# A grouped 3x3 convolution behind three attention blocks: its input strips made by a tripled 1x1 convolution in place of shifted copies

## The reference, cut to what matters

```python
h = lax.conv_general_dilated(x, w1, (1, 1), 'SAME', ...) + b1          # 1x1, 64 -> 128 channels
h = jax.nn.relu(_bn(h, g1, be1, m1, v1))
h = lax.conv_general_dilated(h, w2, (1, 1), 'SAME', ...,
                             feature_group_count=32) + b2              # 3x3, 32 groups of 4 channels
h = jax.nn.relu(_bn(h, g2, be2, m2, v2))
out = lax.conv_general_dilated(h, w3, (1, 1), 'SAME', ...) + b3        # 1x1, 128 -> 64
return jax.nn.relu(out + x)
```

## Time and profile before

| | |
|---|---|
| median of three executions | 128.46 us |
| span of the profiled execution | 125.2 us |
| TensorE, matmul | 105.7 us busy, 84% |
| VectorE | 93.7 us, 75% |
| ScalarE | 68.5 us, 55% |
| GpSimd | 42.7 us, 34% |

### The profile page before, as it was taken

One profiled execution on the slowest core, in us unless ns is written; L12 is line 12 of the kernel. 1 busy time (PEld: TensorE's weight loads), 2 busy tenths in 40 slices (PEclk: granted clock), 3 DMA queues, 4 the chain that ended last, 5 costly groups with the idle time before them and its releaser, 6 DMA issues.

```text
span 125.2 us, 1845 instructions
## 1 busy us (share of the span) xinstructions
PE 105.7 (84%) x600; PEld 64.4 (51%) x600; DVE 93.7 (75%) x246; ACT 68.5 (55%) x164; POOL 42.7 (34%) x43
## 2 busy tenths in 40 slices
PE   4988999899999988599399957998697992998990
PEld 1475957577777775365035634985353530221350
DVE  1078999878888669737979989793878739998733
ACT  3137985687979775637503310025534579986530
POOL 8996004351608217095500079991000000000000
PEclk9999999999999999999999999999999999999999
DMA  3960000000000000000000000000000000000022
GB/s 105 309 280 0 0 0 0 5 5 0 0 0 0 0 5 0 0 0 0 5 0 0 0 3 0 0 0 0 0 0 0 0 5 3 0 0 0 5 84 84
DMA packets 1593, 2.81 MB, mean 22 GB/s; under 512 B 176, under 2 KB 1200, under 8 KB 1584
## 3 DMA queue, kind: packets, MB, share of 16 engines
q1 hardware_dynamic: 1152, 2.02, 4.5%
q10 hardware_dynamic: 432, 0.67, 1.6%
HBM read 2.17 MB, written 0.52 MB: 22 GB/s over the span
## 4 chain that ended last, share of the span: by engine, by line
PE 42%; DVE 29%; ACT 15%; issue 8%; DMA 2%; POOL 1%; ACTq 0%; DVEq 0%
PE bank L913 5%; DVE strips L307 5%; PE bank L883 4%; DVE probn L604 4%; ACT prob L411 4%; PE bank L1074 3%; PE bank L1104 3%; DVE ffh L253 3%; PE bank L1116 3%; PE bank L1052 3%; ACT strips L529 3%; DVE nmax L595 3%; DMA p<-in_p 2%; PE duo L1140 2%; DVE qkprod L738 2%
## 5 line engine op out<-in xcount | busy, mean ns | idle before, releaser
L411 ACT ACTIVATE prob<-bank,nmax 128x256 f32<-128x256 f32 x32 | 14.8, 469 | 8.2 <-DVE nmax L595 7.8
L883 PE MATMUL bank<-kz,q 128*128 128x256 f32 x64 | 16.4, 383 | 0.3 <-ACT kz L400 0.3
L595 DVE TENSOR_REDUCE nmax<-bank 128x2 f32<-128x512 f32 x16 | 11.0, 689 | 5.7 <-PE bank L883 5.7
L307 DVE COPY strips<-strips 32x480 f32<-32x480 f32 x32 | 12.8, 400 | 3.0 <-ACT strips L529 2.4
L883 PEld LDWEIGHTS bank<-kz,q 128*128 128x128 f32 x64 | 11.5, 190 | 2.1 <-issue 0.5
L604 DVE TENSOR_SCALAR probn<-prob,rrec 128x256 f32<-128x256 f32 x32 | 12.1, 421 | 0.6
L529 ACT ACTIVATE strips<-bank,bnsh 32x512 f32<-32x512 f32 x16 | 10.9, 680 | 2.1 <-PE duo L1140 1.1
L893 PE MATMUL bank<-pv,probn 128*128 128x128 f32 x64 | 10.0, 278 | 2.1 <-DVE probn L604 2.1
L501 ACT ACTIVATE sq<-bank,cb 128x512 f32<-128x512 f32 x4 | 2.7, 687 | 15.3 <-PE bank L1074 11.0
L1140 PE MATMUL duo<-strips,ctaps 128*32 128x512 f32 x72 | 8.3, 596 | 3.2 <-DVE strips L307 3.2
L893 PEld LDWEIGHTS bank<-pv,probn 128*128 128x128 f32 x64 | 7.4, 142 | 4.6 <-DVE probn L604 4.2
(11 more groups left out here) (148 smaller groups left out, 229.3 us busy)
## 6 DMA issues: line engine op xcount, KB each, us to landing
p<-in_p SPq DMA_DIRECT2D x1, 952.0 KB, 7.1
xT<-in_xT SPq DMA_DIRECT2D x4, 128.0 KB, 4.0
p<-in_p ACTq DMA_DIRECT2D x1, 448.0 KB, 5.7
out_dram<-xT SPq DMA_DIRECT2D x1, 256.0 KB, 2.0
out_dram<-xT SPq DMA_DIRECT2D x2, 128.0 KB, 1.7
pv<-in_pv ACTq DMA_DIRECT2D x1, 128.0 KB, 3.2
p<-in_p ACTq DMA_DIRECT2D x1, 79.5 KB, 3.0
```

What stands on the lines that cost most here:

```text
L307: return engine.tensor_copy(strips[32 * s:32 * s + 32, c % 2, r, :, 1:1 + SIDE, d], strips[32:64, c % 2, r, :, 1:1 + SIDE, f])
L411: s.activation(prob[:, n % 3, b, :], S_BANK[n % 3][:, b * TOK:(b + 1) * TOK], ACT.Exp, bias=nmax[:, n, b:b + 1], accum_out=rsum[:, n, b:b ...
L595: v.tensor_reduce(nmax[:, n, :], S_BANK[n % 3].rearrange("p (b m) -> p b m", b=BLK), AX.X, ALU.max, negate=True).then_inc(max_ready, 1)
L883: ins = mm(S_BANK[n % 3][:, b * TOK:(b + 1) * TOK], q[:, b * 128:b * 128 + 128], k, start=True, stop=True)
```

## The change

`conv1` now runs in 8 units (group `gr`, block `r`), each of six matmuls: for each `ty` of 0, 1, 2 and each image half `i`, 64 rows of input, 32 output columns (block `r`'s channels) into partitions `32 * ty` of the bank of half `i`. For `ty` 0 and 2 the input is shifted by one image row (16 positions), so 240 of each image's 256 positions are computed. The three partition groups of a bank hold the same channels seen from three rows. The 16 positions per image that no input reaches are filled once with -3e38 by two VectorE memsets in PSUM (`edges`), which the ReLU turns into zero. The strip is then written in one instruction of 96 partitions x 512: half 0 by ScalarE, half 1 by VectorE. `conv2` reads 96 partitions and goes over `tx`, the column, with rows of 16 floats in a pitch of 18. There are four strip buffers now, two of them in tiles of earlier stages. The orders of TensorE, ScalarE and VectorE change as shown.

```diff
-            g.memset(strips[:, :, :, :, :, :].rearrange("p a b c d e -> p (a b c d e)"), 0.0)\
+            g.memset(strips[:, :, :, :, :, 0:PAD:PAD - 1].rearrange("p a b c d e -> p (a b c d) e"), 0.0)\
                 .then_inc(zeroed, 1)
...
+            pool.wait_ge(avsum_sb, len(UNITS))
+            pool.wait_ge(pv_ps, NATT // 2)
+            for c in (2, 3):
+                g.memset(strip_of_chunk[c][:, :, :, :, 0:PAD:PAD - 1].rearrange("p r j a e -> p (r j a) e"), 0.0)\
+                    .then_inc(zeroed, 1)
...
+            def conv1_out(u):                                                  # ScalarE
+                act.wait_ge(c1_ps, u + 1)
+                if u % CONV_BLOCKS == 0:
+                    act.wait_ge(taps_ready, 1)
+                    act.wait_ge(zeroed, 3 if u == 0 else 5)
+                r = u % CONV_BLOCKS
+                s.activation(strip_of(u, 0), image_rows(conv1_bank(u, 0)[0:96, :]), ACT.Relu,
+                             bias=shift3[:, r:r + 1]).then_inc(c1_act, 1)
...
             conv1_out(0)
+            conv1_out(1)
             inverse_std(3)
-            conv1_out(1)
-            conv2_out(0)
             conv1_out(2)
             conv1_out(3)
+            conv2_out(0)
+            conv1_out(4)
+            conv1_out(5)
+            conv1_out(6)
             conv2_out(1)
+            conv1_out(7)
             conv2_out(2)
             conv2_out_last()
...
+            for r in range(CONV_BLOCKS):                                       # VectorE, after c1s
+                for ty in range(3):
+                    v.tensor_copy(shift3[32 * ty:32 * ty + 32, r:r + 1], bnsh[32 * r:32 * r + 32, 0:1])
...
+            def edges():
+                dve.wait_ge(ff_act, 2 * FH)
+                dve.wait_ge(ff_dve, 2 * FH)
+                rows = quad.rearrange("p (b a n) -> p b a n", b=4, a=2)
+                v.memset(rows[0:32, :, :, 0:SIDE], NOTHING)
+                v.memset(rows[64:96, :, :, TOK - SIDE:TOK], NOTHING).then_inc(edge_ps, 1)
+
+            def conv1_out(u):                                                  # VectorE
+                dve.wait_ge(c1_ps, u + 1)
+                if u % CONV_BLOCKS == 0:
+                    dve.wait_ge(zeroed, 3 if u == 0 else 5)
+                r = u % CONV_BLOCKS
+                v.tensor_scalar(strip_of(u, 1), image_rows(conv1_bank(u, 1)[0:96, :]), shift3[:, r:r + 1], 0.0,
+                                ALU.add, ALU.max).then_inc(c1_dve, 1)
...
             relu_ff(1)
+            edges()
             layer_norm(2)
-            shifts(0)
+            for u in range(CONV_BLOCKS):
+                conv1_out(u)
             layer_norm(3)
-            shifts(1)
-            shifts(2)
-            shifts(3)
+            for u in range(CONV_BLOCKS, 2 * CONV_BLOCKS):
+                conv1_out(u)
...
-            def conv1(c):
-                gr, i = c // 2, c % 2
+            def conv1(u):
+
+                gr, r = u // CONV_BLOCKS, u % CONV_BLOCKS
                 pe.wait_ge(ln_out, 3 + gr)
-                if c == 0:
+                if u == 0:
                     pe.wait_ge(taps_ready, 1)
-                    pe.wait_ge(ff_act, 4)
-                    pe.wait_ge(ff_dve, 4)
-                mm(bank[c], c1s[:, i, :], x2[:, gr, :], start=True, stop=True).then_inc(c1_ps, 1)
+                    pe.wait_ge(edge_ps, 1)
+                if u >= 2:
+                    pe.wait_ge(c1_act, u - 1)
+                    pe.wait_ge(c1_dve, u - 1)
+                for ty in range(3):
+                    to = slice(SIDE, TOK) if ty == 0 else slice(0, TOK - SIDE) if ty == 2 else slice(0, TOK)
+                    of = slice(0, TOK - SIDE) if ty == 0 else slice(SIDE, TOK) if ty == 2 else slice(0, TOK)
+                    for i in range(2):
+                        own = slice(64 * i, 64 * i + 64)
+                        o = conv1_bank(u, i)[32 * ty:32 * ty + 32, :].rearrange("p (j n) -> p j n", j=2)
+                        x = x2[own, gr, :].rearrange("p (j n) -> p j n", j=2)
+                        ins = mm(o[:, :, to], c1s[own, i, 32 * r:32 * r + 32], x[:, :, of],
+                                 start=True, stop=True)
+                ins.then_inc(c1_ps, 1)
...
-                pe.wait_ge(shifted, CONV_BLOCKS * (c + 1))
+                pe.wait_ge((c1_act, c1_dve)[c % 2], CONV_BLOCKS * (c // 2 + 1))
...
-                        ins = mm(bank[7 - c % 2][32 * r:32 * r + 32, :], ctaps[:, r, ty, :],
-                                 strips[:, c % 2, r, :, ty:ty + SIDE, :], start=ty == 0, stop=ty == 2)
+                        ins = mm(bank[7 - c % 2][32 * r:32 * r + 32, :], ctaps[0:96, r, tx, :],
+                                 strip_of_chunk[c][:, r, :, :, tx:tx + SIDE], start=tx == 0, stop=tx == 2)
...
             conv1(0)
+            conv1(1)
             variance(3)
-            conv1(1)
-            conv2(0)
             conv1(2)
             conv1(3)
+            conv2(0)
+            conv1(4)
+            conv1(5)
             conv2(1)
-            conv2(2)
+            conv1(6)
+            conv1(7)
             conv3(0, 0)
             conv3(0, 1)
+            conv2(2)
             conv2_last()
```

More of the change, by code:

```diff
@@ L75, in sem @@
             return ctx.enter_context(nc.semaphore(name))
-        low = [ctx.enter_context(nc.psum_tensor(f"bank{i}", [128, 512], F32)) for i in range(6)]
+        quad = ctx.enter_context(nc.psum_tensor("quad", [128, 2048], F32))
+        low = [ctx.enter_context(nc.psum_tensor(f"bank{i}", [128, 512], F32)) for i in range(4, 6)]
         duo = ctx.enter_context(nc.psum_tensor("duo", [128, 1024], F32))
-        bank = [b[:, :] for b in low] + [duo[:, 0:512], duo[:, 512:1024]]
+        bank = [quad[:, 512 * i:512 * i + 512] for i in range(4)] + [b[:, :] for b in low] + \
+            [duo[:, 0:512], duo[:, 512:1024]]
         S_BANK = bank[0:3]
@@ L120, in build @@
         bnsh = sb("bnsh", 128, 2)
+        shift3 = sb("shift3", 96, CONV_BLOCKS)
         xT = sb("xT", 128, PAIRS, TOK)
@@ L168, in build, with strip_view @@
         ffh = sb("ffh", 128, 2, FH, 2, 512)
-        strips = sb("strips", 128, 2, CONV_BLOCKS, 2, PAD, SIDE)
+        strips = sb("strips", 96, 2, CONV_BLOCKS, 2, SIDE, PAD)
+        STRIP = CONV_BLOCKS * 2 * SIDE * PAD
+        def strip_view(ap):
+            return ap.rearrange("p (r j a b) -> p r j a b", r=CONV_BLOCKS, j=2, b=PAD)
+        strip_of_chunk = [strips[:, 0, :, :, :, :], strips[:, 1, :, :, :, :],
+                          strip_view(qkprod[0:96, :, :, :].rearrange("p a k n -> p (a k n)")[:, 0:STRIP]),
+                          strip_view(keys1[0:96, 0:STRIP])]
         products = [qkprod[:, 0, :, :], qkprod[:, 1, :, :]] + [
@@ L302, in flat, with conv1_bank, strip_of, image_rows @@
             return ap.rearrange("p a b -> p (a b)")
[L304 to L308, removed]
+        NOTHING = -3.0e38
+        def conv1_bank(u, i):
+            return bank[2 * (u % 2) + i]
+        def strip_of(u, i):
+            gr, r = u // CONV_BLOCKS, u % CONV_BLOCKS
+            return strip_of_chunk[2 * gr + i][:, r, :, :, 1:1 + SIDE]
+        def image_rows(ap):
+            return ap.rearrange("p (j a b) -> p j a b", j=2, b=SIDE)
         @block.sync
@@ L1137, in conv2 @@
                     pe.wait_ge(c2_sb, c - 1)
-                for ty in range(3):
+                for tx in range(3):
                     for r in range(CONV_BLOCKS):
-                        ins = mm(bank[7 - c % 2][32 * r:32 * r + 32, :], ctaps[:, r, ty, :],
-                                 strips[:, c % 2, r, :, ty:ty + SIDE, :], start=ty == 0, stop=ty == 2)
+                        ins = mm(bank[7 - c % 2][32 * r:32 * r + 32, :], ctaps[0:96, r, tx, :],
+                                 strip_of_chunk[c][:, r, :, :, tx:tx + SIDE], start=tx == 0, stop=tx == 2)
                 ins.then_inc(c2_ps, 1)
             def conv2_last():
-                pe.wait_ge(shifted, CONV_BLOCKS * 4)
+                pe.wait_ge(c1_act, 2 * CONV_BLOCKS)
+                pe.wait_ge(c1_dve, 2 * CONV_BLOCKS)
                 for h in range(2):
-                    for ty in range(3):
+                    for tx in range(3):
                         for r in range(CONV_BLOCKS):
-                            ins = mm(bank[h][32 * r:32 * r + 32, 0:TOK], ctaps[:, r, ty, :],
-                                     strips[:, 1, r, h, ty:ty + SIDE, :], start=ty == 0, stop=ty == 2)
+                            ins = mm(bank[h][32 * r:32 * r + 32, 0:TOK], ctaps[0:96, r, tx, :],
+                                     strip_of_chunk[3][:, r, h, :, tx:tx + SIDE], start=tx == 0, stop=tx == 2)
                     ins.then_inc(c2_ps, 1)
@@ L1257, in packed_inputs @@
                 for g in range(8):
-                    at = 32 * (3 * r + ty) + 4 * g
+                    at = 32 * (3 * r + tx) + 4 * g
                     m = 32 * r + 4 * g
-                    part["ctap"][32 * tx + 4 * g:32 * tx + 4 * g + 4, at:at + 4] = \
```

(1 more changed line is left out.)

27 lines of the change are left out of this document (5 added, 22 removed).

## The result

The changed kernel took 128.97 us in the median of 20 executions (128.41 to 131.05), the kernel before 128.57 beside it. The ratio is 1.0061, 95% interval 1.0033 to 1.0088: slower by 0.6%, where 130.5 us and 1.6% were forecast. The comparisons leave out executions well above a kernel's quickest.

The account below looks back on a forecast made before the run. The stage was taken as bound by moving data between partitions, afterwards by TensorE. +3.44 us tripled convolution, +0.5 `edges` and -1.9 waits gave +2.0 on span 125.2; with 3.3 on top, 130.5 us, range 129.1 to 132.4.

Parts of the forecast that it names:

- `edges`: Two VectorE memsets and their wait before `layer_norm(2)`: 0.5 us on the path, bounds 0.2 and 0.6.
- the last of the sum: Profiled span 125.2 plus 2.0 gives 127.2 us; the 3.3 us the median has on top gives 130.5 us.
- The rounds: TensorE's 512-column instructions on each column group: 0.43 us each, two per `conv1` unit, 0.86 us; this case's chance 0.86.
- rows of 16 cost nothing: `conv2` reading short rows: taken as 0; as a rival 4%, 0.4 us, 130.9 us, its chance within the 0.86.
- the evictions' price: ScalarE and VectorE writing the strips: 680 ns and 0.74 us each, independent of the number of partitions.
- Serial halves: Rival in the `conv1` units: row halves run one after the other, 1.72 us a unit, 136.4 us; chance 0.06.
- shorter rounds: Rival in the eight `conv1` units: 64-row rounds under 0.43 us; 128.5 us at 0.22, 127.4 at 0.11; chance 0.05.
- The schedule: Order of work from `conv1(0)` at 101.05 to `conv2_last` at 120.17 us, which started at 118.15 before: +2.0 us.
- the wait of 1.2: TensorE idle before `conv2(0)`, waiting for ScalarE's `inverse_std(3)` and evictions of units 2 and 3: 1.2 us.
- "Nothing" for the smaller memset: GpSimd's shorter memset at the start: no effect on time, its result being first needed after 109 us.
- The tail gap: TensorE's wait before `conv2(0)`; the forecast counted waits in the whole stage as falling by 1.9 us, from 4.7.
- the sign: Whole kernel slower, chance 0.91; same 0.04, faster 0.05.

Follow-up runs that it names:

- no_edges: The changed kernel without the two VectorE memsets that fill unreached positions, `conv1(0)` waiting for `relu_ff(1)` instead: 128.40 us.
- fill_head: The kernel before with two matmuls of zeros ahead of `head_sums(1)`, in TensorE's wait near 62 us: 128.51 us, ratio 1.0006 to before.
- fill_tail: The kernel before with two matmuls of zeros between `conv1(1)` and `conv2(0)`, where TensorE waited 2.44 us: 128.02 us, ratio 0.9964 to before.
- after_fill_head: The changed kernel with two matmuls of zeros ahead of `head_sums(1)`, in TensorE's wait near 62 us: 128.72 us, ratio 1.0048 to before.
- fill_both: The kernel before with two matmuls of zeros in each wait, ahead of `head_sums(1)` and ahead of `conv2(0)`: 127.01 us, ratio 0.9909 to before.
- after_again: The changed kernel, unchanged, measured again: 129.34 us, ratio 1.0077.
- late_memset: fill_both with the strips' memset moved behind the select on GpSimd: 127.03 us.
- half_columns: The changed kernel with every `conv1` matmul over one image of the two: 127.70 us, ratio 0.9961 to before.
- pool_shift: late_memset with the right shifts of blocks 1 and 3 copied by GpSimd in place of VectorE: 127.21 us, ratio 0.9953.

## Why the prediction was wrong

**The step that failed** is the last of the sum: "The sum is made on the profiled span, 125.2 + 2.0 = 127.2; with the 3.3 us that the median has on top, 130.5 us." It takes the 3.3 us for something that lies around every span and would come along. Only 1.8 of them do. The other 1.5 are one stretch at 1.2 GHz, which the profiled execution did not have and most do. The changed kernel has no such stretch in 23 of its 32 executions, so these 1.5 were not to be added. The trace of before could have raised the question: 3.3 us is much to lie outside a span, and a full clock in all 40 slices stood beside a median of executions of which nothing was known. The account of the error: 130.5, less 1.5 for the stretch, less 0.6 for the span (126.6 against 127.2; 0.4 to 0.5 of it is the memset at the start, 0.1 the schedule), plus about 0.4 of time outside the span, is 128.8.

**By its other steps:**
- The rounds were right. Units of 0.86 with six tiles at once; rows of 16 cost nothing; the evictions' price does not depend on partitions (0.69 and 0.75 with 96). Serial halves and shorter rounds are out.
- `edges`, forecast 0.5: +0.48 in the trace, 0.4 by no_edges.
- The schedule: 19.12 us forecast from `conv1(0)` to `conv2_last`, 19.00 measured. From `conv1(0)` to `conv2(0)` it was 5.65 for 5.80; the wait of 1.2 reads 0.82, and 0.2 of the difference is the tail of the matmul before it, which the trace counts as work. `conv3(0, 1)` is late for ScalarE, as worked out: its weight loads wait 0.4 for it.
- "Nothing" for the smaller memset: wrong by 0.46. I asked who waits for GpSimd, and not whose instruction runs beside it.
- The tail gap: the prediction says "The gaps are worth less than what is put into them." At full clock that is right, +1.4. It priced the gap as idle time alone. The matmuls right behind it were the ones that slowed down, 2.78 to 4.48 us in fill_head.

**Why the sign held.** At full clock the change costs 1.4 us of span and 1.9 of time (128.84 against 126.98). Against that it saves 1.3 us of low clock in the mean, 0.8 of it shown to go with the tail gap (fill_tail) and the rest not explained. What remains is 0.6 to 0.8% in the ratios. With the clock kept up in both kernels the cost is plain: 128.72 (after_fill_head) against 127.01 (fill_both). No term of the prediction foresaw the regained clock, which nearly paid for the added work; that it stayed smaller than the cost, and with it the sign, was partly luck.

**What stays open.** Why, with the head gap open and the tail gap closed, the clock falls in only 4 of 12 executions of after_again, but in 9 of 12 of fill_tail, and whether all of these begin at the head gap. Why a low stretch comes near 90 us in the traces of late_memset and half_columns, where neither differs from its base, and why late_memset has one in 4 of 12 executions with both gaps filled. And the time outside the span: about 1.8 us in before and all its variants but pool_shift (2.3), 2.0 to 2.2 in 17 of the 32 executions of after and 2.4 to 3.1 in the other 15, up to 3.4 in half_columns. The traces end before it, so 0.3 us or more of the change's cost is measured and not explained.

## What to carry to other kernels

Before adding a span difference to a median, take the profiled execution's own time and clock, and ask which executions the median is made of: time outside the span comes along, a stretch at the lower clock may not. Where TensorE waits 2 us or more in a dense kernel, look at how long the same matmuls take behind the wait, and try two matmuls of zeros in each gap before rebuilding the stage; here that was worth 0.9%, and the rebuilt stage cost 0.6%. When a step on an idle engine is made shorter or moved, look at what the other engines run beside it at both places.

## What was not expected of the hardware

- A stretch at the lower level (granted clock 0.50) began within 0.3 us of the first matmul after waits of 2.06, 2.21, 2.43 and 2.44 us in the traces and cost 1.5 to 1.7 us each. With waits of 0.35 to 0.82 at the same places, 21 of 23 executions had none (fill_both, after_fill_head). It also began near 90 us, behind waits of 0.78 and 0.89 only.
- It is not fixed by the program: the same kernel shows none, one, two or three such stretches, in 16, 55, 33 and 16 of 120 executions, if each step of the table above is one stretch.
- Six float32 tiles of 64 rows and 32 columns run at once, in the rounds of 0.43 us of a whole 128 x 128 matmul.
- VectorE's pair of normalisations of 128 x 256, 0.62 us by itself, took 1.08 beside GpSimd's select and 1.72 beside its memset.
